# Layer 3's experts picked by raw logits, four weights instead of thirty-two, and a second queue for the last loads

## The reference

```python
logits = x2d @ gate_w.T
rw = softmax(logits, axis=-1)
scores = sigmoid(logits)
_, sel = top_k(scores, 4)
w = take_along_axis(rw, sel, axis=-1)
w = w / w.sum(axis=-1, keepdims=True)
cw_large[rows, sel] += w
cw_small[rows, sel // 2] += w
large = sum_e (silu(x @ Wg[e]) * (x @ Wu[e]) * cw_large[:, e]) @ Wd[e]
small = the same with cWg, cWu, cWd and cw_small
x = x + tanh(g_ffn[3]) * (large + 0.05 * small)
```

## Time and profile before

| what | value |
|---|---|
| median of 3 runs | 1260.8 us (1259.81 to 1264.31) |
| the profiled execution's own time | 1262.57 us |
| its span, first to last instruction | 1260.3 us |
| mean granted clock of PE in it | 0.915 of full speed |
| PE, DVE, ACT, POOL busy | 84%, 65%, 55%, 54% of the span |
| DMA | 142.13 MB, mean 113 GB/s |

### The profile page before, as it was taken

How to read it: one execution, slowest core, us unless ns; L and a number is a source line. 1 busy time by engine, 2 the same in 40 slices (tenths; PEclk the granted TensorE clock), 3 DMA queues, 4 the chain that set the end, 5 groups by cost and what they waited for, 6 DMA issues and landing times.

```text
span 1260.3 us, 17914 instructions
## 1 busy us (share of the span) xinstructions
PE 1064.4 (84%) x5320; PEld 831.2 (66%) x5320; DVE 818.9 (65%) x1507; ACT 694.2 (55%) x1758; POOL 681.6 (54%) x452
## 2 busy tenths in 40 slices
PE   6576688877756987999999999998989846999993
PEld 3466577766523765888888888765555445888983
DVE  3882799778769761666566656759999485333332
ACT  4466555444456226777777777648655126544441
POOL 2106888888833222344545445429998112787653
PEclk8878799988966998999999999979999957999997
DMA  6494899886550003111011110214343994455445
GB/s 191 148 195 127 237 286 289 240 229 160 95 146 1 1 1 104 55 51 55 18 55 58 49 42 16 72 34 132 122 129 103 209 258 137 65 83 77 55 52 133
DMA packets 139632, 142.13 MB, mean 113 GB/s; under 512 B 33684, under 2 KB 126860, under 8 KB 139540
## 3 DMA queue, kind: packets, MB, share of 16 engines
q1 hardware_dynamic: 115556, 110.71, 30.3%
q0 software_dynamic: 22896, 29.24, 14.5%
q10 hardware_dynamic: 1088, 1.05, 0.3%
HBM read 114.98 MB, written 25.99 MB: 112 GB/s over the span
## 4 chain that ended last, share of the span: by engine, by line
PE 55%; POOL 17%; DVE 10%; issue 8%; DMA 5%; ACT 4%; SPq 0%; ACTq 0%; POOLq 0%; DVEq 0%
PE bank L2489 8%; POOL f_sums L1038 7%; POOL arena L1024 5%; PE bank L1619 4%; PE bank L1704 4%; PE bank L1715 4%; PE bank L1682 4%; PE bank L1637 2%; PE bank L1608 2%; DMA f_sums<-arena,put 2%; PE bank L2146 2%; PE bank L1693 2%; PE bank L2509 2%; PE bank L2507 2%; POOL arena L565 2%
## 5 line engine op out<-in xcount | busy, mean ns | idle before, releaser
L545 DVE TENSOR_TENSOR_SCAN arena<-arena 128x1024 f32<-128x1024 f32 x64 | 155.3, 2426 | 22.4 <-issue 13.2
L1038 POOL DMA_INDIRECT f_sums<-arena,put x64 | 128.2, 2004 | 24.2 <-issue 17.7
L565 POOL TENSOR_TENSOR arena<-arena 128x1024 f32<-128x1024 f32 x32 | 82.5, 2579 | 85.8 <-DVE arena L545 85.8
L2394 POOL DMA_INDIRECT e_sums<-ssm_y,put x63 | 98.4, 1562 | 47.2 <-DVE ssm_y L2701 27.2
L1024 POOL DMA_INDIRECT arena<-y_rows,slots x64 | 84.3, 1317 | 65.3 <-DVEq L1239 46.1
L2489 PE MATMUL bank<-arena,ssm_y 128*128 x504 | 108.8, 360 | 1.4 <-issue 0.7
L523 ACT ACTIVATE arena<-arena,ssm_A 128x255 f32<-128x255 f32 x256 | 108.0, 498 | 0.2
L2146 PE MATMUL bank<-rows,arena 128*128 128x512 f32 (+1 forms) x224 | 103.3, 605 | 3.3 <-ACT arena L2077 3.3
L575 PE MATMUL bank<-arena,ident 128*128 128x256 f32 x256 | 71.5, 428 | 34.1 <-DVE arena L565 33.6
L2695 DVE TENSOR_TENSOR ssm_y<-ssm_y,bank 128x256 f32<-128x256 f32 x63 | 26.5, 421 | 108.9 <-ACT ssm_y L2571 108.9
L534 DVE TENSOR_TENSOR arena<-arena 128x1024 f32<-128x1024 f32 x64 | 94.3, 1473 | 0.0
(11 more groups left out here) (338 smaller groups left out, 2718.0 us busy)
## 6 DMA issues: line engine op xcount, KB each, us to landing
arena<-bc_rows SPq DMA_DIRECT2D x64, 512.0 KB, 5.6
arena<-in_L_ffn_w_gate_dram SPq DMA_DIRECT2D x16, 256.0 KB, 4.0
arena<-in_L_ffn_w_up_dram SPq DMA_DIRECT2D x16, 256.0 KB, 4.5
arena<-in_L_ffn_w_down_dram SPq DMA_DIRECT2D x16, 256.0 KB, 5.7
rows<-in_L_ffn_w_gate_dram SPq DMA_DIRECT2D x16, 256.0 KB, 4.3
rows<-in_L_ffn_w_up_dram SPq DMA_DIRECT2D x16, 256.0 KB, 4.7
rows<-in_L_ffn_w_down_dram SPq DMA_DIRECT2D x16, 256.0 KB, 6.3
arena<-in_L_ffn_Wd_dram SPq DMA_DIRECT2D x1, 3072.0 KB, 18.0
```

The source lines that it names most:

```text
L545: nc.vector.tensor_tensor_scan(ssm_h[:, j % 2, :], ssm_decay[:, j % 2, :], ssm_in, 0.0, ALU.mult, ALU.add).then_inc(s_ssm_h, 1)
L565: ops.tensor_tensor(ssm_hC_buf[:, j % 2, :], ssm_h[:, j % 2, :], ssm_C[:, g % 2, :], ALU.mult).then_inc(s_ssm_hC, 1)
L1038: nc.gpsimd.indirect_dma_start(out=f0_sums[m % SUMS], out_offset=bass.IndirectOffsetOnAxis(ap=put[:, m:m + 1], axis=0), in_=f0_ye[:, n % R ...
L2394: nc.gpsimd.indirect_dma_start(out=e_sums[t % 2], out_offset=bass.IndirectOffsetOnAxis(ap=put[:, t:t + 1], axis=0), in_=e_ye[:, t % 4, :], ...
```

## The change

Experts are picked from the logits as they lie in PSUM: `max` and `max_index` read bank 2 directly. The sigmoid, the scaled logits and the maximum over 32 are gone. `e_wk` now starts as the four best logits less the best one (`g_best` has them already), times `rstd`; ACT takes the exponential of these 128 x 32 values alone. The sum, the reciprocal and the scaling of `e_wk` stand behind the positions' reduction (L2640) instead of ahead of the wait for PE's counts. At the end, SP issues the four loads of the first sum only, and ACT, which waits for the same scatters, those of the second.

```diff
         def e_sp(sp):
...
             for b in range(B):
                 tiles = slice(TPB * b, TPB * (b + 1))
-                for dst, rows in ((x, e_sums[0]), (e_more, e_sums[1])):
-                    sp.dma_start(dst[:, tiles, :], rows[0:T, :].rearrange("(i p) d -> p i d", p=P)[:, tiles, :]
-                                 ).then_inc(s_e_more[b][0], 16)
+                sp.dma_start(x[:, tiles, :], e_sums[0][0:T, :].rearrange("(i p) d -> p i d", p=P)[:, tiles, :]
+                             ).then_inc(s_e_more[b][0], 16)
...
         def e_act(act):
             for b in range(B):
                 rows_turn_act(act, b, 5, (3, 4))
-            wait(act, s_e_top, 1)
-            nc.scalar.activation(e_sig[:, :, :], e_pos[:, :, :], ACT.Exp, scale=-1.0).then_inc(s_e_exp[0], 1)
             act.wait_ge(s_e_new, 1)
-            nc.scalar.activation(e_p[:, :, :], e_p[:, :, :], ACT.Exp).then_inc(s_e_exp[0], 1)
+            nc.scalar.activation(e_wk[:, :, :], e_wk[:, :, :], ACT.Exp).then_inc(s_e_exp[0], 1)
...
             e_steps(step)
+            for r in range(4):
+                wait(act, s_e_st[r], 16 * len(range(r, RUN, 4)))
+            for b in range(B):
+                tiles = slice(TPB * b, TPB * (b + 1))
+                nc.scalar.dma_start(e_more[:, tiles, :], e_sums[1][0:T, :].rearrange("(i p) d -> p i d", p=P)[:, tiles, :]
+                                    ).then_inc(s_e_more[b][0], 16)
...
             wait(dve, s_e_logit, 1)
-            V.tensor_tensor(e_pos[:, :, :], bank[2][:, 0:NT * E3].rearrange("p (i e) -> p i e", i=NT),
-                            rstd[:, :].unsqueeze(2).to_broadcast([P, NT, E3]), ALU.mult).then_inc(s_e_top[0], 1)
-            wait(dve, s_e_top, 1)
-            dve_link(V.tensor_reduce(e_top[:, :], e_pos[:, :, :], AX_X, ALU.max))
-            V.tensor_tensor(e_p[:, :, :], e_pos[:, :, :], e_top[:, :].unsqueeze(2).to_broadcast([P, NT, E3]),
-                            ALU.subtract).then_inc(s_e_new, 1)
-            wait(dve, s_e_exp, 1)
-
-            dve_link(V.tensor_scalar(e_sig[:, :, :], e_sig[:, :, :], 1.0, None, ALU.add))
-            dve_link(V.reciprocal(e_sig[:, :, :], e_sig[:, :, :]))
             for i in range(NT):
-                last = V.max(g_best[:, i, :], e_sig[:, i, :])
+                last = V.max(g_best[:, i, :], bank[2][:, i * E3:(i + 1) * E3])
             dve_link(last)
             for i in range(NT):
-                last = V.max_index(g_idx[:, i, :], g_best[:, i, :], e_sig[:, i, :])
+                last = V.max_index(g_idx[:, i, :], g_best[:, i, :], bank[2][:, i * E3:(i + 1) * E3])
             dve_link(last)
...
             V.tensor_tensor(e_mask, e_eq2[:, :, 0, :], e_eq2[:, :, 1, :], ALU.add).then_inc(s_e_mask[0], 1)
-            wait(dve, s_e_exp, 2)
-            wait(dve, s_e_mask, 1)
-            dve_link(V.tensor_tensor(e_eq2, e_eq, e_p[:, :, :].unsqueeze(2).to_broadcast([P, NT, K3, E3]), ALU.mult))
-            dve_link(V.tensor_reduce(e_wk[:, :, :], e_eq2, AX_X, ALU.add))
-            dve_link(V.tensor_reduce(e_wsum[:, :], e_wk[:, :, :], AX_X, ALU.add))
-            dve_link(V.reciprocal(e_wsum[:, :], e_wsum[:, :]))
-            dve_link(V.scalar_tensor_tensor(out=e_wk[:, :, :], in0=e_wk[:, :, :], scalar=tanh_g[:, 1, 3:4],
-                                            in1=e_wsum[:, :].unsqueeze(2).to_broadcast([P, NT, K3]), op0=ALU.mult, op1=ALU.mult))
+            dve_link(V.tensor_tensor(e_wk[:, :, :], g_best[:, :, 0:K3], g_best[:, :, 0:1].to_broadcast([P, NT, K3]), ALU.subtract))
+            V.tensor_tensor(e_wk[:, :, :], e_wk[:, :, :], rstd[:, :].unsqueeze(2).to_broadcast([P, NT, K3]),
+                            ALU.mult).then_inc(s_e_new, 1)
 
             wait(dve, s_e_rank, 1)
...
             dve_link(V.tensor_reduce(e_locf[:, :, :], e_eq2, AX_X, ALU.add))
+            wait(dve, s_e_exp, 1)
+            dve_link(V.tensor_reduce(e_wsum[:, :], e_wk[:, :, :], AX_X, ALU.add))
+            dve_link(V.reciprocal(e_wsum[:, :], e_wsum[:, :]))
+            dve_link(V.scalar_tensor_tensor(out=e_wk[:, :, :], in0=e_wk[:, :, :], scalar=tanh_g[:, 1, 3:4],
+                                            in1=e_wsum[:, :].unsqueeze(2).to_broadcast([P, NT, K3]), op0=ALU.mult, op1=ALU.mult))
             dve_link(V.tensor_copy(e_loc[:, :, :], e_locf[:, :, :]))
```

More of the change, by code:

```diff
@@ L2300, in flamingo_kernel @@
         e_mask = f0_mask[:, :, 0:E3]
-        e_p = sb("e_p", [P, NT, E3])
         e_sig = sb("e_sig", [P, NT, E3])
         e_pos = sb("e_pos", [P, NT, E3])
-        e_top = sb("e_top", [P, NT])
-        e_sum = sb("e_sum", [P, NT])
         e_wk = sb("e_wk", [P, NT, K3])
@@ L2326, in flamingo_kernel @@
         s_e_pad = sem("s_e_pad")
-        s_e_logit, s_e_top, s_e_exp, s_e_mask, s_e_rank = (
-            (s, 1) for s in (s_f0_logit, s_f0_top, s_f0_exp, s_f0_mask, s_f0_rank))
+        s_e_logit, s_e_exp, s_e_mask, s_e_rank = (
+            (s, 1) for s in (s_f0_logit, s_f0_exp, s_f0_mask, s_f0_rank))
         s_e_yrows, s_e_slots = (s_f0_yrows, 16), (s_f0_slots, 2)
```

## The result

| what | before | after |
|---|---|---|
| median of 6 runs each | 1261.63 us (1255.91 to 1265.1) | 1255.39 us (1251.89 to 1262.62) |
| ratio, with 95% interval | | 0.9948 (0.9923 to 0.9973) |
| profiled execution, its span | 1262.57, 1260.3 us | 1262.62, 1260.7 us |
| end of the logit matmuls in it | 1024.78 us | 1031.18 us |
| from there to the end of the span | 235.52 us | 229.52 us |

The change takes 0.5% off, 6.2 us between the medians; 5.1 was forecast. By the ratio's interval the gain is 3.4 to 9.7 us, so the times alone can't tell 5.1 from 6.2. The two profiled executions have nearly the same span, and a reader who compares spans alone would see nothing. The one of after lost 6.4 us before it came to any changed instruction, 6.0 of them early on: the loads after layer 0, where both kernels have the same code, begin at 361.6 us in it and at 355.6 in the earlier trace rows.

What follows compares the result with a forecast made beforehand. The prediction took DVE's chain from logits to cast as the bound ahead of the experts, and the loads at the end. Gains of 4.5 and 0.6 us, 5.1 off the median 1260.8, gave 1255.7 us, range 1252.2 to 1259.3.

Steps and rivals of the forecast that it cites:

- Ahead of the mask: DVE from logits to mask: scaling, maximum, subtraction, addition, reciprocal and a wait for ACT go, 3.36 us sooner.
- Reading PSUM: Eight maxima and eight index searches reading the bank: cost taken as nothing, at most 1.7 us.
- Behind the mask: DVE from mask to cast: memset 1.45 us behind the mask; with the part before it, cast 4.52 us earlier net.
- The wait for ACT: DVE's new wait for the exponential ahead of the sum: 4 us of slack, so no delay.
- The store of the rows: Rows stored to HBM ahead of POOL's gathers: landing stays hidden, 3.6 us before the slots are ready.
- The end: Last loads issued from SP and ACT: between 2.0 us gained and 0.8 lost, 0.6 gained taken.
- the sum: Whole forecast: 4.5 us from the routing plus 0.6 from the end, 5.1 us gained.
- the rival: Last loads: engines already full, so the second queue brings nothing; 4.5 us gained in all, 1256.3 us, chance 0.25.
- The experts' steps: 65 steps after the placement: unchanged work that only moves, carrying all 4.52 us.
- the clock's: PE's clock over placement and first expert steps: between 2.6 us gained and 3.0 lost, taken as nothing.
- signs of being wrong: Listed signs, among them a clock rising elsewhere than 2.9 us into placement and 5.3 us into the expert steps.
- the slower rival: Clock stays low through the placement and into expert steps: up to 11.3 us lost, 1267.0 us, chance 0.03.

Runs made afterwards that it cites:

- e1_route: The changed kernel with all eight loads of the end on SP's queue again, so the routing part alone; ratio 0.9939 to the kernel before.
- e3_again: The changed kernel run once more, unaltered; ratio 0.9946 to the kernel before.
- e1_sum_early: The changed kernel with sum, reciprocal and scaling of the weights put back ahead of DVE's wait for PE's counts; ratio 0.9943 to the kernel before.
- e2_big: The changed kernel with the end's loads on SP alone, four of 512 KB; wait for the last loads ended 8.39 us behind the first issue.
- e1_end: The kernel before with only the change's end, its loads split between SP and ACT; ratio 0.9995 to the kernel before.
- e2_half: The changed kernel without the second sum's loads, so half the bytes; last addition 5.63 us behind the first issue.
- e1_warm: The changed kernel with 39 added matmuls that nobody reads in PE's idle times; ratio 0.9958 to the kernel before.
- e2_best: The changed kernel with the early sum, POOL's gathers 12 steps ahead instead of 8, and added unread matmuls in larger groups; ratio 0.9915 to the kernel before.

## Why the prediction was right, and where not

- **Ahead of the mask**: 3.36 forecast, 3.29 measured (8.31 to 5.02). The difference is the bank as a source.
- **Reading PSUM**: taken as nothing, bound 1.7. The eight maxima took 0.89 instead of 0.85, the searches 1.44 instead of 1.40: 0.08 us for all, not the 1.0 that was estimated from the Trainium skill's cycle table ("VectorE: DVE Perf Modes", section on the TRN2 errata). The trace disagrees with the page here.
- **Behind the mask**: memset at 1.48 behind the mask (1.45 forecast), cast at 10.89 (10.83). Net 4.46 us against 4.52, and e1_route and e3_again repeat it to a hundredth. e1_sum_early then showed that the 0.78 which the change leaves behind the wait could be had as well.
- **The wait for ACT**: 4.5 us of slack against 4 forecast. Nothing waited.
- **The store of the rows**: POOL's first gather was released by DVE's slots, not by a DMA, as argued. The rows had landed at 1056.11, 3.85 us ahead of the slots (3.6 forecast).
- **The end**: 0.6 forecast, 0.6 found over nine traces, and 0.26 in the one profiled pair. The start was later (first addition 3.67 to 4.60 us behind the issue with two queues, 3.40 and 3.62 with one), the rate higher, both as in the sum. But 0.6 was the middle of two wide ends (2.0 gained, 0.8 lost), so that it came out is in part luck. The reason I gave, that two queues move data faster, was too narrow: e2_big has the rate on one queue. I had also read the earlier trace rows as the same case, though SP issues eight loads there beside ACT's four. Of the rival and its page (the Trainium skill, "DMA: Bandwidth & Descriptors", "Issuing engines are not separate DMA queues"), the claim that a second issuer saves only issue time isn't what the rows show, as the rate in the middle of the stretch rose by a fifth and more, and did so after the last issue too; but it is right that the queue as such isn't needed for it.
- **The experts' steps**: "unchanged work, and they only move" is the step that failed. They came out 1.33 us sooner at the first scatter, more than the whole 6.0 - 5.1 by which the sum fell short; the end gave 0.34 less than its term in this pair. The size is the clock's: I took nothing for it, between 2.6 gained and 3.0 lost, and it gave 1.3 behind the slots and took 0.24 in the placement. A clock that rises elsewhere than 2.9 and 5.3 us into the two was one of my signs of being wrong, and it came, at 3.7 and 2.6. That it came out on the good side is luck as far as the prediction goes, and so is 1255.39 beside 1255.7: the median of before had moved up by 0.8 with the added runs. I had also read the stretch as PE's. It is POOL's up to the last gather, so only what moves the first scatter counts there, and PE's faster steps behind it would not have.
- The point that would have decided for the slower rival, a clock still low when the placement ends, was far off: it rose 3.7 us into it.

## What to carry to other kernels

Count from a point that the change can't reach: here two executions of the same code differed by 6.4 us ahead of it, more than the change is worth, and the stretch from the logits to the cast repeated to a hundredth. Put small work into a wait that the same edit opens; here DVE idled 1.2 us ahead of PE's counts while 0.78 us of it stood just behind them. Where two engines share a loop, compare their periods (3.2 us for POOL, 2.82 for PE) before taking the busier one as the bound, and look for a gap ahead of the loop in which the slower can get ahead. Here one changed number took some 2.6 us of stalls away.

## What the runs showed of the hardware that was not expected

- The clock's falls and rises came at the same place of the program in each trace of the same code. With the old routing (before, e1_end) it rose 2.8 and 2.9 us into the placement and 5.3 and 5.4 us into the expert matmuls; with the new one (after, e3_again, e2_big, e2_half, e1_route) 3.6 to 3.8 and 2.6 to 2.7. Counted from the logits it rose at 21.5 us with the old and at 17.8 to 18.0 with the new, so 3.6 us sooner for a placement that starts 4.5 us sooner. I had treated this as chance that can't take sides; a few microseconds of shift moved it the same way each time.
- PE's short matmuls in idle times raised the clock ahead of the placement in e1_warm and kept it at 1.00 in e2_best, where the gaps behind the placement were filled as well; e1_warm's fewer ones didn't keep it.
- A DMA share of 0.92 to 0.99 stood beside 282 to 289 GB/s with eight loads in one queue, and 1.04 to 1.09 beside 351 to 371 with four to a queue, of 256 KB on two or of 512 KB on one. A share near 1 is no proof that the engines give all they can.
- Three traces (e1_route, e1_sum_early, e1_warm) have a late activation on ACT at the first expert steps, worth 0.7 us and more at the first scatter. It started 1.4 to 2.4 us after the matmuls that it reads had ended. It is not explained.
